# Second expert routing on one Trainium2 core: earlier weight loads, TensorE's low parts ahead of the rank products, eight lane comparisons on ScalarE, and twenty filler products

## The reference

```
# layer 1, attention: 4 heads of 64, softmax over 1024 context rows
x = x + softmax(q k^T * 64**-0.5) v @ Wo          # q from layernorm(x), k and v from the context
# layer 1, experts: 8 of them, 2 for each token
logits = xf @ Wg                                   # xf = layernorm(x), 2048 x 256
top_vals, top_idx = top_k(logits, 2); gate = softmax(top_vals)
comb = (one_hot(top_idx) * gate) * alpha           # weight of each expert for each token
for e in range(8):
    a = gelu((layernorm(xf) * ln_w[e] + ln_b[e]) @ fc1_w[e] + fc1_b[e])    # 256 -> 1024
    out += (a @ fc2_w[e] + fc2_b[e]) * comb[:, e]                          # 1024 -> 256
```

## Time and profile before

| what | us |
|---|---|
| median of 3 runs | 955.72 (954.75 to 956.1) |
| the profiled execution, whole | 951.11 |
| its span, first to last instruction | 949.3 |
| TensorE busy in the span | 875.8 (92%) |
| VectorE, ScalarE, GpSimd busy | 568.0, 487.4, 431.6 |

### The profile page before, as it was taken

How to read it: one execution, slowest core, us unless ns; L and a number is a source line. 1 busy time by engine, 2 the same in 40 slices (tenths; PEclk the granted TensorE clock), 3 DMA queues, 4 the chain that set the end, 5 groups by cost and what they waited for, 6 DMA issues and landing times.

```text
span 949.3 us, 19403 instructions
## 1 busy us (share of the span) xinstructions
PE 875.8 (92%) x6172; PEld 751.9 (79%) x6173; DVE 568.0 (60%) x1292; ACT 487.4 (51%) x1038; POOL 431.6 (45%) x374
## 2 busy tenths in 40 slices
PE   5899999867999998679999999997899999999995
PEld 4698989746899997457777777765599999999994
DVE  7885463485666667566666666687654545445442
ACT  5744231255444453466576665565454554555542
POOL 2473432004555573667264463320444555656532
PEclk9999999978999999899999999997899999999998
DMA  9731000175766755761020000328377667667662
GB/s 308 238 105 41 5 1 1 55 251 175 272 231 232 253 189 168 173 159 48 1 68 23 19 27 1 117 77 273 126 213 213 194 196 208 190 209 203 187 198 27
DMA packets 68609, 134.72 MB, mean 142 GB/s; under 512 B 8096, under 2 KB 50720, under 8 KB 63424
## 3 DMA queue, kind: packets, MB, share of 16 engines
q1 hardware_dynamic: 55200, 110.27, 34.3%
q0 software_dynamic: 13344, 23.63, 11.2%
HBM read 109.08 MB, written 21.64 MB: 138 GB/s over the span
## 4 chain that ended last, share of the span: by engine, by line
PE 63%; DMA 5%; DVE 4%; POOL 3%; issue 2%; ACT 2%; SPq 0%; POOLq 0%; DVEq 0%; ACTq 0%
PE d_hps L1995 15%; PE d_yps L2005 7%; PE b_hps L1995 7%; PE c_av L1022 5%; PE c_tp L1010 5%; PE c_sc L997 4%; PE c_xb L946 4%; PE d_yps L2008 4%; PE b_yps L2005 3%; PE b_yps L2008 2%; PE c_xb L1031 1%; DMA d_w<-in_w 1%; PE c_xb L969 1%; DMA x<-k_rows 1%; PE d_take L1984 1%
## 5 line engine op out<-in xcount | busy, mean ns | idle before, releaser
L1892 ACT ACTIVATE x<-d_hps,b 128x128 f32<-128x128 f32 x312 | 89.2, 368 | 120.5 <-PE d_hps L1995 119.4
L1995 PEld LDWEIGHTS d_hps<-d_xg_t,d_xw 128*128 128x128 f32 x1248 | 147.8, 195 | 1.4
L1995 PE MATMUL d_hps<-d_xg_t,d_xw 128*128 128x128 f32 x1248 | 148.0, 278 | 0.0
L905 POOL TENSOR_SCALAR c_prob<-c_prob,c_rinv 128x1024 f32<-128x1024 f32 x64 | 72.3, 1146 | 108.0 <-DVE c_rinv L1365 107.6
L2005 PE MATMUL d_yps<-d_w,d_hid_hi 128*128 x312 | 115.2, 402 | 0.0
L1802 POOL DMA_INDIRECT out_x<-d_y,d_take_slot x39 | 63.2, 1619 | 99.4 <-DVE d_y L2220 92.5
L1358 DVE CUSTOM_DVE_ANT_0 c_prob<-c_sc,c_minf 128x1024 f32<-128x1024 f32 x64 | 75.7, 1219 | 29.0 <-PE c_sc L997 26.8
L2183 DVE TENSOR_SCALAR d_xg_t<-d_take,ln_w,ln_b 128x128 f32<-128x128 f32 x78 | 28.5, 406 | 92.0 <-PE d_take L1984 91.9
L2008 PE MATMUL d_yps<-d_w,d_hid_lo 128*128 x312 | 81.2, 281 | 0.0
L1010 PE MATMUL c_tp<-const,c_prob 128*128 128x128 f32 x512 | 70.6, 281 | 10.6 <-DVE c_pt L1370 5.2
L1995 PEld LDWEIGHTS b_hps<-b_xg_t,b_w 128*128 128x128 f32 x624 | 76.7, 195 | 2.9 <-issue 1.3
(11 more groups left out here) (370 smaller groups left out, 2063.1 us busy)
## 6 DMA issues: line engine op xcount, KB each, us to landing
d_xw<-in_w SPq DMA_DIRECT2D x39, 1024.0 KB
b_w<-in_w SPq DMA_DIRECT2D x47, 512.0 KB, 3.6
d_w<-in_w SPq DMA_DIRECT2D x8, 1024.0 KB, 8.3
a_raw<-in_ctx_t SPq DMA_DIRECT2D x8, 512.0 KB, 7.2
a_raw<-in_ctx SPq DMA_DIRECT2D x8, 512.0 KB, 4.4
ybuf<-a_zero SPq DMA_DIRECT2D x2, 2048.0 KB, 12.6
k_stage<-in_ctx_t SPq DMA_DIRECT2D x12, 256.0 KB, 3.1
rows<-b_xn_all SPq DMA_DIRECT2D x1, 2048.0 KB, 12.4
```

Of the source, the lines that this page charges most:

```text
L905: nc.gpsimd.tensor_scalar(prob[w][:], prob[w][:], rinv[:, w:w + 1], 1.0, ALU.mult, ALU.mult).then_inc(s["prob_ready"], 1)
L1892: op = nc.scalar.activation(hid[q][:, h * FH + c, :], src[:, c, :], ACT.Gelu_apprx_tanh, bias=b1[:, ds(e, 1), h * FH + c])
L1995: mm = nc.tensor.matmul(hps[j % 2][h][:, c * P:(c + 1) * P], w1[j % WL][:, k, at:at + P], xg_t[j % 2][:, k, :], start=(k == 0), stop=(k == ...
```

## The change

Seven edits, all for the second layer (`first` is False):

- `prob` and `v` change places in the attention's memory, so that expert 5's w2 lies over prob0 and prob1 instead of v.
- SyncE loads experts 4 and 5 together, after the maxima and after the turning of all probabilities but the last unit's two (`tp_hi`). Only 6 and 7 wait for the last product with the values.
- TensorE turns pairs 6 and 7 two iterations ahead like the others, and ScalarE does `high(5)` after pair 4 instead of after pair 5.
- `low_parts(6)` on TensorE moves ahead of the wait for d_load and the rank products, and `low_out(6)` on ScalarE ahead of exp.
- `low_out(7)` precedes both of ScalarE's value parts.
- LANES_ACT becomes 8: the last eight lane matrices are made by ScalarE.
- Twenty filler products instead of eight follow the d_slots products.

```diff
-FREE_FIRST = 4
-LAST_LOW = (5, 6, 7)
+FREE_FIRST = (4, 5)
+LAST_LOW = (6, 7)
...
+        prob = [sb(f"prob{q}", [P, M]) for q in range(4)]
         v = sb("v", [P, JC, H, HD])
-        prob = [sb(f"prob{q}", [P, M]) for q in range(4)]
...
             sp.wait_ge(s["max_done"], B * UP * 2)
-            m.load_w2(sp, FREE_FIRST)
+            sp.wait_ge(s["tp_hi"], B * UP * 2 - 2)
+            for n in FREE_FIRST:
+                m.load_w2(sp, n)
...
-    HIGH_AT = (1, 3, 5, 7) if first else (2, 5)
-    LANES_ACT = 8 if first else 0
+    HIGH_AT = (1, 3, 5, 7) if first else (2, 4)
+    LANES_ACT = 8
...
             for e in PE_LOW:
                 high(act, e)
+            if not first:
+                low_out(PE_LOW[0])
             act.wait_ge(s["routed"], ROUTED["exp_in"])
...
-            for e in PE_LOW:
-                low_out(e)
-                if e == PE_LOW[1 if first else 0]:
-                    value_parts()
+            if first:
+                for e in PE_LOW:
+                    low_out(e)
+                value_parts()
+            else:
+                low_out(PE_LOW[1])
+                value_parts()
...
-                if i + AHEAD < (PAIRS if first else PAIRS - AHEAD):
+                if i + AHEAD < PAIRS:
                     turn_pair(i + AHEAD)
-                if not first and i == PAIRS - AHEAD:
-                    for late in range(i, PAIRS):
-                        turn_pair(late)
                 logits(i)
                 warm(1, rank)
 
+            if not first:
+                low_parts(PE_LOW[0])
             pe.wait_ge(s["routed"], ROUTED["load"])
...
-            for e in PE_LOW:
-                low_parts(e)
+            if first:
+                for e in PE_LOW:
+                    low_parts(e)
+            else:
+                low_parts(PE_LOW[1])
...
-            warm(8, rank)
+            warm(8 if first else 20, rank)
```

## The result

The changed kernel took 948.12 us in the median of 4 runs (947.27 to 950.87) against 955.24 (952.84 to 956.1) for the kernel before: ratio 0.9935, 95% interval 0.9917 to 0.9952.

A forecast was written before the change was run, and what follows sets the result against it. The prediction held TensorE to bound the kernel from 690 us on, so an earlier or faster-clocked start of the blocks counts almost whole: -1.1 and -2.4 make -3.5, from 955.7 to 952.2 us, range 950.5 to 955.0.

The forecast's parts named there:

- Loads, pairs, `high(5)`: Second routing: expert 5 loaded earlier, TensorE doesn't stop after pair 5, last logits at 652.1 against 654.29, -2.2 us.
- Expert 6's low part ahead of the ranks: Before the rank products: piece 2 waits behind `high(7)`, costing 1.2 us, so -1.0 of the shift stands.
- Eight lanes: Lane matrices before the slots: eight moved to ScalarE, slots read at 671.7, -0.6 us here, -1.6 in sum.
- A: Rival at the rank products: expert 7's weights land no earlier; 955.0 us, or 953.6 at half the delay; chance 0.17.
- C: Rival at `up`: fillers don't hold the clock, `up` runs at half clock, only -1.1 left, 954.6 us; chance 0.09.
- D: Rival, slower: rank products wait for expert 7; gain gone from landing at 656.5, 957.7 us at 658.5; chance 0.06.
- B: Rival: clock falls before `low_parts(6)`, ranks read 1.5 us later, -2.0, or 953.7 us; chance 0.13.
- Twenty fillers: Behind the slots: clock back after 4.0 us, first block waits 1.0, `up` starts -1.1 us instead of -1.6.
- my lower bound of 2.7: Shortest assumed time from the fillers' begin to the clock's return, taken from the first routing; gives `up` -1.6 us.
- `up` at full clock: First 64 products of `up`: the clock holds, 7.46 us instead of 9.84, -2.4 us.
- The step from the trace to the median: Whole kernel: distance of 4.6 us from profiled execution to median kept, turning 947.6 into 952.2 us.
- first step: Second routing: new loads, pairs and earlier `high(5)` bring the last logits 2.2 us earlier.

The follow-up runs named there:

- r5: Kernel before with only the new loads, exchanged tiles, pairs 6 and 7 turned ahead and `high(5)` after pair 4: 949.58 us against 954.04, ratio 0.9951.
- r9: Kernel before with the new loads, exchanged tiles, pairs, earlier `high(5)` and twenty fillers, without the low-part and lane edits: 948.77 us, ratio 0.9933.
- r2: Changed kernel, nothing edited, run again beside the kernel before: 949.78 us in the median of 12, ratio 0.9944.
- r15: Kernel before, nothing edited, one more trace; its profiled execution took 956.12 us.
- r12: Kernel before with only the attention tiles prob and v exchanged in memory: 953.79 us against 953.72, ratio 0.9996.
- r8: Changed kernel plus eighteen filler products on TensorE between expert 7's low part and the slots: 949.68 us, ratio 0.9939.

## Why the prediction was wrong: its size

Means over the four traces of before and the five of the change, beside the forecast:

| mark | before | changed | moved | forecast |
|---|---|---|---|---|
| last logits | 14.2 | 11.6 | -2.6 | -2.2 |
| ranks read | 19.2 | 17.9 | -1.3 | -1.0 |
| slots | 33.8 | 31.9 | -1.9 | -1.6 |
| `up` begins | 39.8 | 37.8 | -1.9 | -1.1 |
| block 2 | 52.3 | 48.1 | -4.2 | -3.5 |

*Loads, pairs, `high(5)`: right.* In the first traces -2.2 exactly (13.57 to 11.37); 0.4 more in the mean, because in two of four traces of before the clock falls before the last logits are done. I had read one in which it fell just behind them.

*Expert 6's low part ahead of the ranks: right.* Expert 7's weights came as reckoned from expert 6's old place, piece 2 waited 1.17, VectorE 1.50; 1.2 lost was the forecast. Without this edit (r5, r9) the ranks come at 16.4 to 16.6.

*Eight lanes: right*, 0.5 from ranks to slots (14.6 in before, 14.05 in the first trace of the change) against 0.6. Rivals A, C and D did not come: expert 7's weights landed 12.4 after the last projection's end (653.84 - 641.45), where expert 6's had landed before (653.04 - 640.72 = 12.3), and expert 6's were there by 650.56, when `high(6)` began without a wait. The Trainium skill, DMA: Bandwidth & Descriptors, section "Queues, rings and completion order", says that completion is not FIFO per issuing engine; in this trace the two loads landed in order all the same. B came in full in one of five traces, at 1.9 instead of 1.5.

*Twenty fillers: mis-sized.* I let the clock come back 4.0 us after they began, so that they held the first block for 1.0 and `up` for 0.5. It came back after 2.35 in the first trace, below my lower bound of 2.7; they ended at 677.41, and the first block came 4.36 after the slots mark against 4.22 in the first trace of before, so they held it 0.1; in the five traces it was 0.0 to 0.7. `up` also stands behind the second block's turn, whose place my sum carried over from before:

```profile
679.48 0.69 PE L1984 MATMUL d_take<-const,d_xg 128*128 128x128 f32 x2 [0.93 <-DMA d_xg<-rows,d_take_slot]
```

That is before; after the change the turn ran at full clock (678.49, 0.44) and came 0.1 sooner after the slots. So `up` moved by 1.9 instead of 1.1, 0.5 of it for the hold and 0.3 for the second block, and the sum is -4.3 instead of -3.5.

*`up` at full clock: right*: -2.4 was forecast, the first traces show 9.84 to 7.41.

*The step from the trace to the median: this failed.* The profiled execution itself was forecast at 947.6 and took 947.27, in part by luck: the routing gave 0.8 more than the sum, and the attention ended 0.7 later. The 4.6 us from there to the median, which I carried over as a constant, was 0.85 in the first four runs of the change (948.12 - 947.27) and -2.9 in r2 (949.78 - 952.70). It is no property of the kernel: the 951.11 of before that it was counted from is as short as only four of 119 timed executions.

Most of that shortness lay ahead of the place that the change touches. The same row of the second layer's scores (the second group) in the first trace of before and in r15, the same program:

```profile
386.36 0.50 PE L997 MATMUL c_sc<-c_k_hi,c_q_hi 64*128 64x512 f32 x2 [2.67 <-DVE c_nmax L1358]
...
390.76 0.50 PE L997 MATMUL c_sc<-c_k_hi,c_q_hi 64*128 64x512 f32 x2 [2.67 <-DVE c_nmax L1358]
```

The 18 traces of this study reach it at 385.5 to 392.9 us (mean 388.5) and take 251.4 to 254.7 from it to the last projection's start (mean 253.1). The first trace of before is 2.1 and 0.7 under these means, and in the routing 0.3 under the mean of its own kernel. Neither stretch favours the change: 387.7 and 253.0 in the mean over the four traces of before, 388.5 and 253.5 over the five of the change.

By their medians the three comparisons give 7.1, 5.8 and 7.5 us; pooled they are 955.6 (59 executions of before) and 949.7 (22 of the change), 6.0 us, of which the traces show 4.2 in the routing. The remaining 1.8, and more in the first four runs, no trace places: the blocks don't make it (256.2 to 256.8 in all), for the exchanged tiles r12 sees no difference, and with standard deviations of 1.5 to 2.8 us between executions and few traces chance can make it; that is not shown.

Against each other, first step and fillers carry the gain: alone 4.5 and 2.6, together (r9) as much as the whole change. The low part ahead of the ranks costs more than the lanes bring at the slots (31.9 in the mean against 31.0 and 31.2 in r9 and r5, one trace each), but in the timed executions the version without both (r9) is not told apart from the change.

## What to carry to other kernels

Before a profiled execution serves as the zero of a sum, set it beside the timed ones: here only four of 119 were as short, and its distance to the median did not carry over to the changed kernel. Where a clock can fall in a hand-over, reckon each term at both clock levels. Judge by timed executions whether parts add up, not by one trace: r9's trace, of the slowest of nine executions, lost clock in `up`, while its median held the 4.5 and 2.6 us of its two parts.

## What the hardware showed unexpectedly

TensorE's clock fell under an engine that the profile, which models the ends of the products, calls fully busy. In r8 the slices from 650 and 651 show TensorE busy 1.00, with logits of eight columns and a filler between them, at a granted clock of 0.92 and then 0.50:

```profile
650.00:651.00 1.00, 1.00 (x11) 0.92 1.07 362
651.00:652.00 1.00, 1.00 (x6) 0.50 1.09 382
```

In other executions of the same rows it stayed at 1.00 (the first trace of the change). Where it falls changes from execution to execution: the stretch up to the second layer's second group of scores scatters over 7.4 us (385.5 to 392.9) and its attention over 3.3 (251.4 to 254.7), in programs that differ there only in the placement of two tiles and, at the attention's end, in the loads. In five traces of that attention read in slices of 10 us the granted clock was 0.66 to 1.00 from 390 to 440 us, and 1.00 behind.
